# A pair of tiles gathered with 12 columns in place of 14, and the wide rows in four groups in place of three

## The reference

```python
def _L0_gnn_ref(x, adj, W, a):
    h = x @ W
    s_src = h @ a[:128, 0]
    s_dst = h @ a[128:, 0]
    e = jax.nn.leaky_relu(s_src[:, None] + s_dst[None, :], negative_slope=0.2)
    e = jnp.where(adj > 0, e, jnp.float32(-9000000000000000.0))
    return jax.nn.softmax(e, axis=1) @ h

h = jnp.maximum(_layernorm(x, axis=-1), 0.0)
return x + _L0_gnn_ref(h, adj, W, a)        # x [8192, 128], adj [8192, 8192] int32
```

## Time and profile before

| | us |
|---|---|
| median of 3 runs | 806.46 (806.06 to 806.75) |
| the profiled execution | 803.09 |
| its span | 801.3 |

### The profile page before, as it was taken

One profiled execution on the slowest core, in us unless ns is written; L12 is line 12 of the kernel. 1 busy time (PEld: TensorE's weight loads), 2 busy tenths in 40 slices (PEclk: granted clock), 3 DMA queues, 4 the chain that ended last, 5 costly groups with the idle time before them and its releaser, 6 DMA issues.

```text
span 801.3 us, 8973 instructions
## 1 busy us (share of the span) xinstructions
PE 516.1 (64%) x1855; PEld 233.0 (29%) x1855; DVE 602.0 (75%) x3125; ACT 527.0 (66%) x371; POOL 512.4 (64%) x522
## 2 busy tenths in 40 slices
PE   3786566677667667666657766676766666756521
PEld 3762223233222233232222222232322122222221
DVE  7957568766876768777779778777776798768984
ACT  3889667676766667676767767677666767676300
POOL 4753776665657665677667666656777656667771
PEclk9799756656765675876785676667667677676655
DMA  8999999999999999999999999999999999999410
GB/s 333 424 393 407 401 403 410 407 406 413 405 407 413 404 407 394 405 396 400 390 400 404 390 402 410 395 409 398 390 382 403 380 406 396 404 380 385 137 37 15
DMA packets 40904, 299.31 MB, mean 374 GB/s; under 512 B 11053, under 2 KB 14035, under 8 KB 24465
## 3 DMA queue, kind: packets, MB, share of 16 engines
q1 hardware_dynamic: 22976, 276.83, 85.5%
q0 software_dynamic: 15328, 17.58, 7.0%
q10 hardware_dynamic: 2544, 4.33, 1.6%
HBM read 304.31 MB, written 8.65 MB: 391 GB/s over the span
## 4 chain that ended last, share of the span: by engine, by line
DMA 70%; ACT 10%; issue 8%; DVE 8%; PE 3%; POOLq 0%; ACTq 0%; DVEq 0%
DMA adj_buf<-in_adj 69%; ACT mask_buf L467 9%; DVE x_all L821 3%; PE banks L1018 1%; DVE stats L560 1%; PE banks L1049 1%; ACT work L431 1%; PE banks L1008 1%; DMA x_all<-in_x 1%; ACT gathered L446 0%; DVE mv_all L564 0%; ACT work L441 0%; DVE newton L577 0%; DVE newton L579 0%; DVE rstd L581 0%
## 5 line engine op out<-in xcount | busy, mean ns | idle before, releaser
L467 ACT ACTIVATE mask_buf<-adj_buf,minus_half 128x2048 bf16<-128x2048 int32 x252 | 490.4, 1994 | 205.9 <-DMA adj_buf<-in_adj 205.4
L361 POOL DMA_INDIRECT gathered<-table,index x448 | 448.3, 1001 | 242.1 <-issue 145.5
L1049 PE MATMUL banks<-mask_buf,bit_ident 128*128 128x512 bf16 x1024 | 388.9, 528 | 103.5 <-ACT mask_buf L467 102.7
L1049 PEld LDWEIGHTS banks<-mask_buf,bit_ident 128*128 128x128 bf16 x1024 | 107.9, 124 | 329.2 <-ACT mask_buf L467 191.6
L821 DVE SCALAR_TENSOR_TENSOR x_all<-gathered,weight,x_all 128x128 f32<-128x128 f32 x512 | 157.7, 348 | 7.2
L636 DVE MAX8 words<-banks 128x8 f32<-128x512 f32 x64 | 44.7, 699 | 122.6 <-PE banks L1049 122.6
L1047 PE MATMUL banks<-key_rows,ones_b 3*128 3x512 bf16 x64 | 32.3, 504 | 124.0 <-ACT mask_buf L467 123.5
L1090 PE MATMUL banks<-x_all,one_hot 128*128 128x128 f32 x128 | 42.5, 433 | 17.5 <-DVE x_all L821 17.4
L1047 PEld LDWEIGHTS banks<-key_rows,ones_b 3*128 3x128 bf16 x64 | 6.1, 95 | 145.7 <-ACT mask_buf L467 144.2
L640 DVE MAX8 words<-rest 128x8 f32<-128x512 f32 x64 | 44.5, 695 | 2.2
L638 DVE MATCH_REPLACE8 rest<-words,banks 128x512 f32<-128x512 f32 x64 | 43.6, 681 | 0.0
(11 more groups left out here) (162 smaller groups left out, 536.1 us busy)
## 6 DMA issues: line engine op xcount, KB each, us to landing
adj_buf<-in_adj SPq DMA_DIRECT2D x128, 2048.0 KB, 18.7
gathered<-table,index POOLq DMA_INDIRECT x448, 6.4
table<-gathered ACTq DMA_DIRECT2D x4, 1040.0 KB, 14.7
x_all<-in_x SPq DMA_DIRECT2D x3, 1024.0 KB, 11.0
out<-x_all SPq DMA_DIRECT2D x2, 1280.0 KB, 23.2
x_all<-in_x SPq DMA_DIRECT2D x2, 512.0 KB, 5.3
out<-x_all SPq DMA_DIRECT2D x1, 1024.0 KB, 26.3
w_gathered<-table,w_index POOLq DMA_INDIRECT x24, 5.8
```

The source lines that it names most:

```text
L361: nc.gpsimd.indirect_dma_start(g_cols[buf][:, k, :], None, table, bass.IndirectOffsetOnAxis(index[:, buf, k:k + 1], 0), bounds_check=N, oo ...
L467: nc.scalar.activation(mask_buf[:, u], adj_buf[:, u], ACT.Sign, bias=minus_half[:]).then_inc(mask_ready, 1)
L1049: ins = mm(bank, bit_ident[:, h * PART_BITS + c], mask_buf[:, u, c * BIT_COLS:(c + 1) * BIT_COLS], start=False, stop=(h == PARTS - 1 and c ...
```

## The change

A pair of tiles has 12 gather columns: four own for each tile, and four shared. Tile 1 now uses the shared columns from the far end: its fifth neighbour wants the last of the four, its eighth the first, so that a column is wanted by both tiles in one partition only where the pair has more than twelve neighbours in its sixteen slots. The wide rows are finished in four groups, which end with batches 7, 15, 23 and 31. One small reduction is added to each batch, since the largest moved neighbour no longer stands first; and `unfit` gets four cells for the moved ones.

```diff
-GROUP_ENDS = (9, 19, 31)
+GROUP_ENDS = (7, 15, 23, 31)
...
-GROUP_STARTS = (0, 10, 20)
+GROUP_STARTS = (0, 8, 16, 24)
...
-OWN = 6
+OWN = 4
...
+        moved_top = sb("moved_top", [P, 1], f32)
...
-        sums_banks = (5, 1, 5)
+        sums_banks = (5, 1, 5, 1)
...
-                    done.add(v.tensor_tensor(both[:], valid[:, par, 0, OWN:], valid_b[:], ALU.mult))
+                    done.add(v.tensor_tensor(both[:, ::-1], valid[:, par, 0, OWN:], valid_b[:, ::-1], ALU.mult))
...
-                    v.tensor_tensor(valid[:, par, 1, 0:SHARED], valid_b[:], both[:], ALU.subtract)
+                    v.tensor_tensor(valid[:, par, 1, 0:SHARED], valid_b[:, ::-1], both[:, ::-1], ALU.subtract)
...
-                    v.tensor_tensor(index[:, par, OWN:SLOTS], mine[:, 0], mine[:, 1], ALU.min).then_inc(index_ready, 1)
+                    v.tensor_tensor(index[:, par, OWN:SLOTS], mine[:, 0], mine[:, 1, ::-1], ALU.min).then_inc(index_ready, 1)
...
+                if hi == BATCH:
+                    v.tensor_reduce(moved_top[:], moved[:], AX.X, ALU.max)
...
-                v.tensor_tensor(ninth[:, 1:2], top[:, 1, SLOTS:SLOTS + 1], moved[:, 0:1], ALU.max)
+                v.tensor_tensor(ninth[:, 1:2], top[:, 1, SLOTS:SLOTS + 1], moved_top[:], ALU.max)
```

More of the change, by code:

```diff
@@ L168, in gat_kernel @@
         max_sum = sb("max_sum", [P, BUFS, BATCH, 2], f32)
-        unfit = sb("unfit", [P, 5, BATCH], f32)
+        unfit_cells = sb("unfit_cells", [P, 4 * BATCH + SHARED], f32)
+        unfit = unfit_cells[:, 0:4 * BATCH].rearrange("p (k b) -> p k b", b=BATCH)
+        unfit_moved = unfit_cells[:, 4 * BATCH:]
         unfit_top = sb("unfit_top", [P, 1], f32)
         zeros = sb("zeros", [P, SUMS], f32)
-        unfit_all = sb("unfit_all", [P, 5, BATCH], f32)
+        unfit_all = sb("unfit_all", [P, 4 * BATCH + SHARED], f32)
         unfit_n = sb("unfit_n", [P, 1], i32)
@@ L544, in _ @@
             v.memset(mean_row[:], 0.0)
-            v.memset(unfit[:], 0.0)
+            v.memset(unfit_cells[:], 0.0)
             done.add(v.memset(minus_half[:], -0.5))
@@ L739, in make_records @@
                     dve.wait_ge(records_added, i - BUFS + 1)
-                last_two = slice(WIDE - SHARED, WIDE)
-                v.tensor_tensor(ninth[:, 1:2], top[:, 1, SLOTS:SLOTS + 1], moved[:, 0:1], ALU.max)
+                last_shared = slice(WIDE - SHARED, WIDE)
+                v.tensor_tensor(ninth[:, 1:2], top[:, 1, SLOTS:SLOTS + 1], moved_top[:], ALU.max)
                 v.tensor_copy(ninth[:, 0:1], top[:, 0, SLOTS:SLOTS + 1])
@@ L744, in make_records @@
                 v.tensor_copy(rec[:, ring, 1, 0:MORE - SHARED], top[:, 1, SLOTS:WIDE - SHARED])
-                v.tensor_tensor(rec[:, ring, 1, MORE - SHARED:MORE], top[:, 1, last_two], moved[:], ALU.max)
-                v.scalar_tensor_tensor(unfit[:, 4], top[:, 1, last_two], float(EXP_BIAS), both[:], ALU.is_ge, ALU.mult)
+                v.tensor_tensor(rec[:, ring, 1, MORE - SHARED:MORE], top[:, 1, last_shared], moved[:], ALU.max)
+                v.scalar_tensor_tensor(unfit_moved, top[:, 1, last_shared], float(EXP_BIAS), both[:], ALU.is_ge, ALU.mult)
                 v.tensor_copy(rec[:, ring, :, REC_S], sd_all[:, i * BATCH:(i + 1) * BATCH, 0])
@@ L751, in make_records @@
                 v.tensor_scalar(is_wide[:, ring], ninth[:], float(EXP_BIAS), None, ALU.is_ge).then_inc(wide_flagged, 1)
-                done.add(v.tensor_tensor(unfit_all[:], unfit_all[:], unfit[:], ALU.max))
+                done.add(v.tensor_tensor(unfit_all[:], unfit_all[:], unfit_cells[:], ALU.max))
             def place_wide(i):
@@ L924, in _ @@
             alone(place_wide(LAST))
-            done.add(v.tensor_tensor(unfit_all[:], unfit_all[:], unfit[:], ALU.max))
+            done.add(v.tensor_tensor(unfit_all[:], unfit_all[:], unfit_cells[:], ALU.max))
             settled()
-            done.add(v.tensor_reduce(unfit_top[:], unfit_all[:], AX.XY, ALU.max))
+            done.add(v.tensor_reduce(unfit_top[:], unfit_all[:], AX.X, ALU.max))
             settled()
```

## The result

The changed kernel takes 808.91 us (median of 20 runs, 806.88 to 810.80), the kernel before in the same comparison 805.44 us (20 runs, 803.72 to 809.05). The ratio is 1.0037, with a 95% interval from 1.0028 to 1.0047: 3.0 us slower by the ratio, 3.5 us by the two medians. The forecast was 805.4 us, within 0.2% of before, with 808.6 us as the upper end of the range. It started from the median of three runs, 806.46 us, which is 1.0 us above that of the 20 runs.

What follows compares the result with a forecast made beforehand. DMA engines bound the load phase, some 740 us, and DVE the tail. Span 801.3 - 4.0 (fewer gathers) + 3.0 (DVE later) = 800.3 us; median 806.46 - 1.0 = 805.4 us, 8-in-10 range 803.0 to 808.6.

Steps and rivals of the forecast that it cites:

- What bounds the kernel: Whole run: DMA engines set the pace for some 740 us; in the some 60 us of tail, DVE's lateness counts.
- The end behind DVE: After DVE's last work: PE's last sums, last `wide_sum` and final store move by DVE's delay, 3.0 us later.
- The sign that it gave for itself: Batch 31's first search to the end: takes the 61.2 us of before and 0.1 more.
- The gathers' price: Load phase: 50 fewer indirect DMAs at 0.08 us each end the loads 4.0 us earlier, between 1.3 and 4.5.
- Bounds of 0.026 and 0.089: Price per indirect DMA in us: lower from q0's excess time over q1's pace, upper from the load rate's shortfall, 400 against 425 GB/s.
- DVE's delay: Batches 29 and 30: the third group's wide steps exceed DVE's idle time, making it 3.0 us later through the tail.
- ACT's new wait: Before the last unit's mask: ACT stands some 2.6 us at `softmax(29)`, covered by 0.3 us; as slower rival 4, 2%.
- Rival 3: Load phase: skipped rows cost nothing, gathers little; at 0.026 us the gain is 1.3 us, total 808.2 us; chance 15%.
- The sign that was to tell it: End of load phase: loads ending less than 1.4 us earlier would show rival 3 right.
- The count of wide rows: Counted in the adjacency: 90, 82, 86 and 78 wide rows in four groups, 80, 65 and 80 in three; limit 128.

Runs made afterwards that it cites:

- fifth experiment: Four all-out-of-bounds gathers behind each of 23 batches (92), added to a 12-column, three-group kernel leaving out its last 11 wide rows; 809.26 us, ratio 1.0043.
- fourteenth: Changed kernel with two empty gathers added behind each of batches 0 to 30, 62 in all; 812.13 us, ratio 1.0091 to the kernel before.

## Why the prediction was wrong

**What bounds the kernel: right.** The load phase ends with the DMA engines, and the tail is DVE's. The tail between the last search and the DRAIN took 41.7 us before and after.

**The end behind DVE: the step that failed.** The prediction said that PE's last sums, the last `wide_sum` and the final store are released by DVE and so move by the same amount. They do; but behind the final store POOL's DRAIN ends the program, and it took 3.1 us more. The sign that it gave for itself was that from the first search of batch 31 to the end the 61.2 us of before pass, and 0.1 more; it was 64.1 us. In the profile before, the term was there to be read, as the 5.9 us between the end of POOL's last instruction (794.45 + 0.98 us) and the end of the span, and no price was given to it. Without this term the change would have come out even, within some 0.5 us.

**The gathers' price: right in kind, too high.** Taken was 0.08 us for 50 gathers, 4.0 us. Measured were 0.060 us (fifth experiment) and 0.068 (fourteenth), 3.0 and 3.4 us for 50; the 62 columns came to 3.9 and 2.7 us with four and with three groups, 3.1 and 2.2 us for 50. All are single comparisons, the best of them good to a third. Bounds of 0.026 and 0.089 held them. The upper one booked the whole shortfall of the rate to the gathers. The lower one counted only the queue's own time, which is what the fifth experiment shows in q0 (0.02 us); that the loads beside it become slower was left out of it. The Trainium skill's figure (DMA: Bandwidth & Descriptors, Bandwidth), some 10.5 ns for a packet, would give an estimated 0.021 us, taken as the time of one engine for each of its two packets. The growth of q0 agrees with it, 0.02 us for a gather; the measured price in device time is three times that.

**DVE's delay: right.** 1.77 and 4.28 us against 1.75 and 1.52 us of idle time gave 3.0 us. Measured as the distance from unit 6's mask to the last search it was 3.05 us; in all ten profiles with the third group's steps at this place it lies between 2.3 and 3.7, 3.0 in the mean. ACT's new wait, forecast at 2.6 us, was 2.67, and covered.

**Rival 3 had the sign, and not the cause.** It put the loss down to gathers that cost little; they cost some 0.06 us, the price at which it said itself that the change comes out even. That its 808.2 us lies near the measured 808.91 is luck: it is a loss of 1.7 us on a start that was 1.0 us too high. The sign that was to tell it, loads that end less than 1.4 us earlier, was met in the two profiles (0.4 us), and misled: one execution of each kernel can't tell 1.4 us here.

**The count of wide rows was wrong.** A row pair in which both tiles have a wide row had been counted once. By the recount the groups of the changed kernel have 99, 88, 97 and 87 wide rows, those of before 84, 68 and 83. The argument stands, as all are under 128, but three groups would not hold them: the last would have 139. The 136 wide rows more agree with the 0.10 MB more in q0: 0.14 MB for their x and their results, less 0.03 for the rows that are no longer skipped.

In one sum: +3.0 us for DVE, +3.1 for the DRAIN and, at 0.060 us, -3.0 for 50 gathers make 3.1 us; measured 3.0 by the ratio and 3.5 by the medians. Against the forecast of -1.0 the DRAIN is the larger part of the miss, 3.1 us, and the gathers' price the smaller, 1.0.

## What to carry to other kernels

Follow the chain of waits past the last useful instruction: the closing barrier is part of the time, and its DRAIN on the engine that issues indirect DMAs moved here by as much as the change gained. Work that hides under waits in a steady phase has to end before that phase does, so look whether the profile shows idle time at their size at the place where a group's closing steps will stand. And price an instruction that looks empty by adding many of it: 92 idle gathers gave a price, to a third, that no row of the trace before held.

## What the runs showed of the hardware

- An indirect gather with all 128 indices out of bounds has the same 32 packets as any other, moves about 4 bytes for each skipped row, and made a saturated load stream 0.060 us longer (0.04 to 0.08; a second comparison gave 0.068). Its own packets account for some 0.02 us of this.
- POOL's last DRAIN took 6.2 to 10.3 us, repeated to 2 ns in one program (9.943 and 9.945 us), and went on for 2.5 to 6.7 us after SP had seen the last store done. An indirect DMA shortly before the end added 0.06 to 0.09 us to it; 16 empty ones far ahead took 0.98 us away, and four changed nothing.
